# Later bias additions, scatters from the first turn, an early table of constants and a later function table in a fused attention and mixture-of-experts kernel

## The reference

```python
x = L0_attn_x                                   # (4, 512, 256), f32
xn = _layernorm(x, axis=-1)
x = x + attn(xn, Wq, Wk, Wv, Wo, bo) + ffn(xn, router_w, router_bias, wg, wu, wd, swg, swu, swd)
# attn: 16 query heads of 16, one key/value head, rotary on 8 dims, causal window of 64
out = softmax(q @ k.T * scale + mask) @ v;  attn = out @ Wo + bo
# ffn: 64 experts of width 64, the best 4 for each token, and 2 shared experts of width 256
_, topk_idx = jax.lax.top_k(logits + router_bias, 4)
routed = einsum('ne,nef,efd->nd', comb, silu(g) * u, wd)
shared = einsum('nsh,shd->nd', silu(sg) * su, swd)
```

## Time and profile before

| | us |
|---|---|
| median of 3 runs | 405.93 |
| lowest and highest of the 3 | 404.23, 411.58 |
| span of the profiled execution, first to last instruction | 407.3 |
| busy: PE, POOL, DVE, ACT | 354.1, 257.5, 248.5, 189.3 |

### The profile page before, as it was taken

How to read it: one execution, slowest core, us unless ns; L and a number is a source line. 1 busy time by engine, 2 the same in 40 slices (tenths; PEclk the granted TensorE clock), 3 DMA queues, 4 the chain that set the end, 5 groups by cost and what they waited for, 6 DMA issues and landing times.

```text
span 407.3 us, 8670 instructions
## 1 busy us (share of the span) xinstructions
PE 354.1 (87%) x2711; PEld 259.3 (64%) x2711; DVE 248.5 (61%) x717; ACT 189.3 (46%) x359; POOL 257.5 (63%) x522
## 2 busy tenths in 40 slices
PE   6698487988976899899999999999999997989753
PEld 3696355665654556448889999999974544545442
DVE  4668877877876878624554645454444419375676
ACT  3485667686766677533455555555532111010100
POOL 5677986777777665022446566877837757667560
PEclk9969989898999889957999999999999999999969
DMA  8940144444484446545988873577974324434341
GB/s 255 213 109 1 54 131 146 131 146 133 161 241 150 142 146 176 156 141 134 296 263 269 267 249 132 181 244 233 337 252 120 105 85 129 128 94 129 103 129 52
DMA packets 73037, 66.81 MB, mean 164 GB/s; under 512 B 9054, under 2 KB 68702, under 8 KB 72994
## 3 DMA queue, kind: packets, MB, share of 16 engines
q1 hardware_dynamic: 66433, 49.30, 40.8%
q0 software_dynamic: 6144, 16.79, 13.0%
q10 hardware_dynamic: 416, 0.18, 0.2%
HBM read 36.78 MB, written 29.23 MB: 162 GB/s over the span
## 4 chain that ended last, share of the span: by engine, by line
PE 64%; DVE 15%; another core or an unknown queue 8%; issue 5%; ACT 4%; DMA 2%; POOL 1%; SPq 0%; DVEq 0%; ACTq 0%; POOLq 0%
PE bank L650 14%; PE bank L675 8%; PE bank L589 8%; PE bank L515 5%; PE bank L624 4%; PE bank L540 4%; PE bank L609 4%; DVE xall L1092 3%; PE bank L436 3%; PE bank L491 3%; DVE xall L1324 3%; PE bank L417 3%; PE bank L523 2%; PE bank L458 1%
## 5 line engine op out<-in xcount | busy, mean ns | idle before, releaser
L1500 POOL DMA_INDIRECT xs_d<-spare,slot_i x64 | 64.2, 1003 | 29.3 <-PE bank L515 7.5
L1593 POOL DMA_INDIRECT wall<-y_d,y_row x64 | 61.4, 959 | 33.7 <-issue 18.3
L1519 POOL COPY spare<-wall 128x256 f32 x127 | 46.9, 400 | 29.9 <-PE bank L650 18.0
L650 PE MATMUL bank<-xall,spare 128*128 x508 | 64.1, 279 | 0.2
L1284 DVE TENSOR_TENSOR spare<-bank,spare 64x512 f32<-64x512 f32 (+1 forms) x64 | 44.1, 690 | 31.0 <-ACT spare L896 30.1
L650 PEld LDWEIGHTS bank<-xall,spare 128*128 128x128 f32 x508 | 59.4, 192 | 2.8 <-issue 0.7
L589 PE MATMUL bank<-xnT,xall 128*128 128x512 f32 x128 | 57.7, 594 | 0.5 <-issue 0.5
L908 ACT ACTIVATE spare<-bank 128x512 f32<-128x512 f32 (+1 forms) x62 | 33.7, 593 | 29.5 <-PE bank L675 17.9
L847 ACT ACTIVATE xall<-bank 98x1024 bf16<-98x1024 bf16 x32 | 32.7, 1021 | 22.6 <-PE bank L436 14.5
L855 ACT ACTIVATE xall<-bank 128x512 f32<-128x512 f32 x64 | 36.6, 601 | 12.5 <-PE bank L491 7.4
L609 PE MATMUL bank<-xall 128*128 128x256 f32 x128 | 32.0, 400 | 11.6 <-DVE xall L1309 8.3
(11 more groups left out here) (172 smaller groups left out, 656.0 us busy)
## 6 DMA issues: line engine op xcount, KB each, us to landing
y_d<-spare SPq DMA_DIRECT2D x31, 512.0 KB, 4.1
wall<-in_wg SPq DMA_DIRECT2D x16, 256.0 KB, 4.8
wall<-in_wu SPq DMA_DIRECT2D x16, 256.0 KB, 5.0
wdn<-in_wd SPq DMA_DIRECT2D x16, 256.0 KB, 4.5
spare<-xs_d SPq DMA_DIRECT2D x32, 128.0 KB, 2.8
small<-xs_d SPq DMA_DIRECT2D x32, 128.0 KB, 3.3
wall<-in_x SPq DMA_DIRECT2D x4, 512.0 KB, 5.7
base_d<-spare SPq DMA_DIRECT2D x16, 128.0 KB
```

The costliest lines, as they stand in the source:

```text
L650: ins = pe.matmul(up_bank_of(G)[:, j * P:(j + 1) * P], wcur[i % NW][:, c * 2 * F:(c + 1) * 2 * F], x_half[c][:, bass.ds(o, P)], start=c == ...
L1500: pool.indirect_dma_start(out=xs_d, out_offset=bass.IndirectOffsetOnAxis(ap=slot_i[:, T, k:k + 1], axis=0), in_=x_n[b][:, t, :], in_offset ...
L1519: pool.tensor_copy(wcur[i % NW].rearrange("p (c g f) -> p c g f", c=NC, g=2), wall[:, bass.ds(o, WE)].rearrange("p (g c f) -> p c g f", c= ...
L1593: pool.indirect_dma_start(out=yk[:, T, k, :], out_offset=None, in_=of, in_offset=bass.IndirectOffsetOnAxis(ap=y_row[:, T, k:k + 1], axis=0 ...
```

## The change

POOL: `add_bias(0)` and `add_bias(1)` now stand behind `rotate_whole(4)`; those for batch 2 are laid between four scatters of turn 0, and those for batch 3 between the scatters of turns 12 and 13. Scatters are now four in each of turns 0 to 11, six in turns 12 and 13, and four in turn 14. SP: `picks` moves to the first slot of `kN` (the spread keys of batch-first tiles), free once the scores of tile 12 are done, and is loaded in turn 14 behind the expert weights and ahead of `store_base(12)`. ACT: the load of Silu's table stands behind `turn(3)`, `attention(14)` and `turn(5)`.

```diff
-    picks = yb[0][0:MROWS * NQG, 0:2, :].rearrange(...)
+    picks = kN[0:MROWS * NQG, near_of(NT - TPB)]
+    PICKS_AT = NT - 2
-    SCATTERED_AT = lambda T: 5 if T <= 11 else 4
+    SCATTERED_AT = lambda T: 6 if T in (NT - 4, NT - 3) else 4
@@ scalar
-        act.activation(unread[:, :], ident[:, 0:1], ACT.Silu)
         turn(3)
         attention(NT - 2)
         turn(5)
+        act.activation(unread[:, :], ident[:, 0:1], ACT.Silu)
         turn(7)
@@ gpsimd
                 pool.tensor_tensor(x_in[b][:, t, :], x_in[b][:, t, :], bo_sb, ALU.add).then_inc(s["x_bo"], 1)
+                yield
-        add_bias(0)
         rotate_whole(0)
...
         rotate_whole(4)
-        for b in range(1, B):
-            add_bias(b)
+        add_bias_whole(0)
+        add_bias_whole(1)
         slots = scatter()
         for T in range(NT):
-            pieces = rotate(T + TPB) if 0 < T < NT - TPB else iter(())
-            if T:
+            if T == 0:
+                pieces = add_bias(2)
+                for i in range(SCATTERED_AT(T)):
+                    next(slots)
+                    next(pieces)
+            else:
+                if T < NT - TPB:
+                    pieces = rotate(T + TPB)
+                elif T == NT - TPB:
+                    pieces = add_bias(B - 1)
                 for i in range(SCATTERED_AT(T)):
...
-                        pool.wait_ge(s["weighted"], QB * (T - 1) + i - 2)
+                        pool.wait_ge(s["weighted"], QB * (T - 1) + min(i, 4) - 2)
                     next(slots, None)
-                    next(pieces, None)
+                    if T < NT - TPB or i in (0, 4):
+                        next(pieces, None)
@@ sync
             if T == NT - 1:
                 sp.wait_ge(s["scattered"], NT * TOPK * 16)
-                sp.dma_start(b16_bits(picks...), edges[...]).then_inc(s["picks"], 16)
                 load_blocks(0, NX)
...
+            if T == PICKS_AT:
+                sp.wait_ge(s["by_key"], XT(NT - TPB))
+                sp.dma_start(b16_bits(picks...), edges[...]).then_inc(s["picks"], 16)
             if 1 < T < NT - 1:
                 store_base(T - 2)
```

9 lines of the change are left out of this document (5 added, 4 removed).

## The result

The median of four executions is 392.38 us (389.51 to 395.24), beside 408.12 us for the kernel before in four executions on the same chip. The ratio is 0.968, with a 95% interval from 0.960 to 0.977.

A forecast was written before the change was run, and what follows sets the result against it. PE held 64% of the critical chain, with waits at the start and hand-over and 13.7 us at half clock. Gains of 1.8 + 0.6 + 0.7 = 3.1 us from 405.93 gave 402.8 us, range 396.5 to 407.0.

The forecast's parts named there:

- Scatters from turn 0: POOL's scatters in the turns: covered by turns of at least 7.1 us, so free; otherwise ACT waits 1 to 2 us.
- rival C: POOL's backlog in turns 12 to 14 delays the first expert block; slower, 407.6 us; chance 0.08.
- The start: Batch 0's additions leave POOL's start; ACT's cast and PE's batch 2 transposes come 1.8 us earlier, bounds 0 and 2.78.
- The clock's share: PE's clock from 20 to 28 us may not fall with less idling: 0.6 us gained, bounds 0 and 2.0.
- Rival B: DVE's routing in turns 0 and 1 ends where it did; only 0.7 us gained, 405.2 us; chance 0.12.
- The clock at the hand-over: From turns to experts, PE's clock stays up once the gap goes; 5.0 of 6.8 us gained, 397.8 us; chance 0.32.
- rival A: PE's clock holds from turns to experts instead of halving for 13.7 us; 5.0 us gained, 397.8 us; chance 0.32.
- the clock fell soon behind the gap: Argument for PE's clock holding: it fell at 173.8, 1.2 us behind the 0.90 us gap before the last scores.
- The tail of the scatters: Last scatter ends at 170.5, first expert block lands at 176.1, before PE wants it at 177.43; cost 0.
- `picks`: Loaded in turn 14, it shrinks PE's gap before the last tile's scores from 0.90 to 0.2: 0.7 us gained.
- The table: Silu's table load on ACT, moved behind three copies: 0 both ways, bounds 1.46 us either way.
- The `near` copies: DVE copies beside POOL's additions, one 908 ns against a median of 327: change 0, bounds -0.6 and +1.2 us.

The follow-up runs named there:

- five_again: Changed kernel with five scatters in each of turns 0 to 11 and four in turn 12, instead of four and six: 408.49 us, ratio 1.008.
- after_again: The changed kernel, unchanged, in a later set of runs: 396.95 us, ratio 0.981 to the kernel before.
- fifth_extra_again: Changed kernel plus a fifth scatter in turns 1 to 11 to an unread DRAM tensor, run where standstills occur: 410.31 us, ratio 1.012.
- adds_moved: Changed kernel with batch 3's four additions one each in turns 8 to 11, not turns 12 and 13: 372.84 us, ratio 0.997; repeated 373.23, 0.998.
- fifth_as_work: Changed kernel plus two unread GpSimd memsets ending each of turns 1 to 11, no added DMA: 378.88 us, ratio 1.012; repeated 379.34, 1.015.
- before_again: The kernel before, unchanged, in a later set of runs: 406.38 us, ratio 0.998.
- p1_start: Kernel before with only batch 0's four additions moved from the start to the other twelve: 404.97 us, ratio 0.994.
- p3_picks: Kernel before with only the `picks` table moved to its new place and turn 14: 407.88 us, ratio 1.001.
- p2_scatters: Kernel before with only the new scatter schedule and batches 2 and 3's additions laid between scatters; batch 0's stay at the start: 402.61 us, no ratio.
- fifth_as_bytes: Changed kernel plus the fifth scatter's 128 KB a turn written by a plain SP DMA in turns 1 to 11: 374.68 us, ratio 1.000.
- p4_table: Kernel before with only the load of Silu's table moved behind three copies: 406.44 us, ratio 0.999.
- fifth_extra: Changed kernel plus a fifth scatter in turns 1 to 11 to an unread DRAM tensor, run where nothing stood still: 380.95 us, ratio 1.018.

## Why the prediction was wrong, and where it was right

**The step that failed** is "Scatters from turn 0", which ended: "then four scatters a turn instead of five, and POOL catches up in turn 3. Free." That PE's turns don't wait for POOL, as the text on rival C says, is true of the semaphores. But five scatters a turn in place of four cost turns 4 to 11 9.4 us in the traces of before and after, 11.4 between five_again and after_again, 9.2 between fifth_extra_again and after_again. The forecast looked only for who waits for POOL. The rows to ask were the turns' own lengths: in the kernel before, turns 4 to 11 do nearly the same work and took from 7.8 to 10.4 us, where adds_moved takes 7.5 to 8.0. The 7.1 us of turns 12 and 13, which the forecast used as a bound, do not show the price of the fifth scatter, though these turns have four: they hold less work (by the stage rows DVE was busy for 5.5 us a turn there and 6.7 before), and in adds_moved they took 7.1 and 7.2 with six.

**A second term missed in the other direction:** turns 12 to 14, for which the text only counted the scatters' own time, lost 3.7 us, with DVE and POOL in standstills of 3.0 and 1.0 us. Over the traces with standstills the kernels with six scatters in turns 12 and 13 take 24.3 to 28.9 us for this stage, those with four 20.7 to 23.5, and the kernel before's 20.7 is the lowest of these. The additions' own time is small: without standstills the stage takes 20.8 without additions in it (adds_moved) and 21.3 with them (fifth_as_work). Whether the additions between the scatters add to the standstills isn't shown, as adds_moved was never run beside them.

**The start** was right in its mechanism. The cast went from 17.44 to 15.36 (forecast 15.6), and PE took up batch 2 1.8 us earlier, as summed (20.70 to 18.89). The clock's share was undersized for this trace: 0.6 was taken, with 2.0 as its bound, and 3.3 - 1.8 = 1.5 came in by the first turn. But after_again ran at half clock for 6.8 us from 20.7, as before_again did from 20.8, and its first turn began 2.1 us earlier. p1_start, where the start stands alone, gives 2.4 us by its ratio. Rival B, the gain taken up again, did not come.

**The clock at the hand-over** was rival A, and its number came in: 15.3 us for the stage in place of 20.9, 5.6 for a forecast 5.0. Its step "the clock fell soon behind the gap" fits the other traces. In five the gap ahead of these scores is 0.74 to 1.34 us (before, before_again, p3_picks, p2_scatters, fifth_as_bytes), and in each the granted clock goes to half within 1.6 us of its end. In twelve it is 0.71 us or less and PE doesn't wait for the first block, and the clock stays up in this stage; p4_table, with a gap of 0.43, took 14.9. In the last three the clock falls beside the longer wait for the first block. That the fall comes with the gap is read from these traces; no run changed the gap alone. Two things in the 5.6 are luck. The gap did not go by the move of `picks`, which alone left 0.74 of it, but by the late signals of turns 14 and 15. And the fall lasted 13.7 us in the trace shown but 3.4 in before_again, where the stage took 16.9; beside that the gain is 1.6. The Trainium skill (TensorE: Matmul & The Clock Gate, "The HAM clock gate"), whose rule was weighed there, has a count that runs free of the kernel, by which one program can fall differently from run to run; these two traces agree. As the comparison of medians averages over such falls, only a part of the 5.6 belongs to the ratio.

**The tail of the scatters** was right: the last one was issued at 155.18, 0.6 us into turn 15, and PE had no gap ahead of L625; nor had it in adds_moved, without standstills. Rival C did not come, but its mechanism is real; fifth_as_work and fifth_extra pay 6.3 and 8.9 us for it.

**`picks`** is worth no more than the interval: 1.001 alone. The forecast had the gap shrink from 0.90 to 0.2 by this move; alone it left 0.74, as SP came to the new place only 0.5 us sooner and the load took 4.0 us to land in place of 3.6. **The table** is worth nothing, as forecast. **The `near` copies** stayed as they were: their longest is 909 ns after, 908 in the earlier trace rows.

**What stays open.** Why engines receive PE's signals late beside scatters is open. The traces have no late signal beside GpSimd's copies, which points to the indirect DMA, but no run with more of GpSimd's time was made where standstills occur. Whether it is the number of scatters or how close they stand is open too, as no kernel changed the one without the other, and so is why it happens in some sets of runs and not in others on the same chip. Where it doesn't happen, the kernels nearest to the changed one that were run, adds_moved twice, gained 0.3% and 0.2%, with 1.000 and 1.001 as upper ends of the intervals; the changed kernel itself was not run there. No version was shown to beat it where standstills occur.

## What to carry to other kernels

Before costing a move at "free because nobody waits for that engine", take the length of each turn of a loop: here turns of nearly the same work took from 7.8 to 10.4 us in the trace of before, and neither ACT nor DVE waited for POOL in them. Compare only turns that hold the same work. Have few indirect DMAs in a turn, and do not catch up by six in a row. Take what a fall of the clock costs from more than one trace: in two traces of one kernel the fall behind the same gap lasted 13.7 and 3.4 us. When a wait goes away, look whether your edit moved what ended it. And a gain that comes from a disturbance is only there when the disturbance is; run such a kernel in more than one set before its number is trusted.

## What the runs showed of the hardware that was not expected

Engines stood for a signal of PE whose matmul was long recorded, for up to 5.8 us in the turns (ACT in fifth_extra_again), and in the last stage three times for about 14 us (ACT 41.9 us before and 42.2 after, three waits each). In the turns 850 of PE's 2906 recorded signals came late in the traces where this happens, nearly all from matmuls that ended during or just behind a scatter, and none of the 4680 of the other engines. In the last stage POOL issues gathers 1.25 us apart, again with nothing between. The same kernel before took 404 to 408 us in four sets of runs and 374 us in two others, one chip giving both. The last stage accounts for 14 of these 31 us (108.5 against 94.3), and turns 4 to 11 for some ten, if fifth_extra_again against fifth_extra (69.6 against 59.9) is taken as the measure. The mean time of a packet of the scatters' queue in the turns is 121 to 127 ns where standstills occur and 124 to 126 where they don't, so the transfers themselves are not slower.
